# Order of the quarter passes in the retention's score and value products

## The reference

```python
Q, K, V = split_heads(x @ Wq), split_heads(x @ Wk), split_heads(x @ Wv)
G = swish(x @ Wg + bg)
Dmask = gammas[:, None, None] ** maximum(diff, 0.0) * causal
scores = einsum('bhtd,bhsd->bhts', Q, K) / scale
ret = einsum('bhts,bhsd->bhtd', scores * Dmask[None], V)
out = layernorm(ret) * G @ Wo + bo
```

## Time and profile before

| | |
|---|---|
| median of 3 runs | 860.75 us (856.7 to 864.1) |
| profiled execution, span from first to last instruction | 858.2 us |
| its mean granted TensorE clock | 0.968 of full speed |
| PE busy | 786.9 us |
| DVE busy | 556.3 us |
| ACT busy | 331.6 us |
| POOL busy | 241.1 us |
| last stage, eight tiles | from about 597 us to the end |

### The profile page before, as it was taken

The page is one execution under the profiler, slowest core; times in us unless marked ns, Lnnn a source line. Parts: engine busy times, 40 slices in busy tenths (PEclk is TensorE's granted clock), DMA queues, the critical chain, the costliest instruction groups (busy, mean ns, idle before and its releaser), DMA issues.

```text
span 858.2 us, 17840 instructions
## 1 busy us (share of the span) xinstructions
PE 786.9 (92%) x6824; PEld 658.3 (77%) x6824; DVE 556.3 (65%) x1364; ACT 331.6 (39%) x692; POOL 241.1 (28%) x182
## 2 busy tenths in 40 slices
PE   4999999996798988989889999999999999999985
PEld 2798988985687777877778989887877777777742
DVE  6545454548766776567675545458657878787875
ACT  2434645452342332433333434354324334432332
POOL 2431212108655645556453101000211011101010
PEclk9999999997998999999889999999999999999998
DMA  8042333330220211302001011164100000000001
GB/s 277 17 157 80 110 118 105 124 104 0 88 93 28 76 43 64 102 28 76 28 28 54 28 55 28 45 232 159 50 1 1 13 12 12 0 12 12 1 0 37
DMA packets 34101, 53.63 MB, mean 62 GB/s; under 512 B 2561, under 2 KB 23297, under 8 KB 32801
## 3 DMA queue, kind: packets, MB, share of 16 engines
q1 hardware_dynamic: 29168, 36.05, 13.2%
q0 software_dynamic: 3328, 16.78, 5.7%
q10 hardware_dynamic: 1584, 0.53, 0.3%
HBM read 51.19 MB, written 2.16 MB: 62 GB/s over the span
## 4 chain that ended last, share of the span: by engine, by line
PE 74%; issue 11%; DVE 9%; ACT 4%; DMA 1%; DVEq 0%; POOL 0%; POOLq 0%; SPq 0%; ACTq 0%
PE bank L228 47%; PE bank L385 6%; PE bank L394 4%; DVE probs L1069 3%; PE bank L548 3%; PE bank L564 3%; PE bank L513 2%; PE bank L408 2%; ACT probs L676 2%; PE bank L501 2%; ACT kT_high L671 1%; DVE kT_low L1059 1%; PE bank L489 1%; PE bank L557 1%; DMA stage<-in_w_xo 1%
## 5 line engine op out<-in xcount | busy, mean ns | idle before, releaser
L228 PE MATMUL bank<-ctx_high,wk_high 128*128 128x258 f32 x512 | 144.1, 282 | 0.5 <-DVE kT_low L1059 0.5
L228 PE MATMUL bank<-ctx_low,wk_high 128*128 128x258 f32 x512 | 144.3, 282 | 0.0
L228 PE MATMUL bank<-ctx_high,wk_low 128*128 128x258 f32 x512 | 143.9, 281 | 0.0
L1069 DVE TENSOR_SCALAR probs<-probs,rrow 128x257 f32<-128x257 f32 x128 | 120.9, 987 | 2.3
L1059 DVE SCALAR_TENSOR_TENSOR kT_low<-bank,bxk,kT_high 128x258 fp32r<-128x258 f32 x128 | 61.8, 483 | 87.8 <-ACT kT_high L671 87.8
L228 PE MATMUL bank<-wv_high,ctx_high 128*128 128x512 f32 x256 | 110.9, 433 | 0.0
L228 PE MATMUL bank<-wv_low,ctx_high 128*128 128x512 f32 x256 | 105.2, 411 | 0.0
L228 PE MATMUL bank<-wv_high,ctx_low 128*128 128x512 f32 x256 | 104.9, 410 | 0.0
L681 ACT ACTIVATE vals<-bank 128x512 f32<-128x512 f32 x64 | 38.3, 598 | 155.7 <-PE bank L228 155.7
L228 PEld LDWEIGHTS bank<-ctx_high,wk_high 128*128 128x128 f32 x512 | 96.7, 189 | 0.8 <-DVE kT_low L1059 0.7
L228 PEld LDWEIGHTS bank<-ctx_low,wk_high 128*128 128x128 f32 x512 | 96.7, 189 | 0.0
(11 more groups left out here) (206 smaller groups left out, 1657.3 us busy)
## 6 DMA issues: line engine op xcount, KB each, us to landing
raw<-in_ctx_t SPq DMA_DIRECT2D x32, 514.0 KB, 4.0
stage<-in_w POOLq DMA_DIRECT2D x16, 1024.0 KB, 5.9
X<-in_x SPq DMA_DIRECT2D x4, 512.0 KB, 7.2
v_last<-last_values SPq DMA_DIRECT2D x32, 64.0 KB
out<-X SPq DMA_DIRECT2D x8, 256.0 KB, 2.0
stage<-in_w_xq SPq DMA_DIRECT2D x1, 1024.0 KB, 8.5
stage<-in_w_xk SPq DMA_DIRECT2D x1, 1024.0 KB, 13.8
stage<-in_w_xv SPq DMA_DIRECT2D x1, 1024.0 KB, 5.5
```

What stands on the lines that cost most here:

```text
L228: last = pe.matmul(to, left(i, c), right(j, c), start=(c == 0 and i + j == 0), stop=(c == C - 1 and i == 1))
L1069: dve.tensor_scalar(probs[:, g, :], probs[:, g, :], rrow[:, g:g + 1], None, ALU.mult).then_inc(probs_ready, 1)
```

## The change

In `retention_scores` the loop over j goes inside the loop over g, so that consecutive matmuls use different row quarters of the array and different banks, and `s_ready` rises four times at the end, in the round g = 3. The wait for `qkv_kept` (bank 3 free, v kept) that stood before j = 2 stands ahead of all of them. In `retain` the loop over j goes inside too, so that consecutive matmuls use different column quarters, and the four waits for `s_decayed`, one ahead of each group, become one wait for the fourth. The arithmetic of each head is the same.

```diff
--- before.py
+++ after.py
@@ -493,22 +493,22 @@
 
                 pe.wait_ge(tqT_kept, t + 1)
                 pe.wait_ge(tkT_kept, t + 1)
-                for j in range(HG):
-                    if j == 2:
-                        pe.wait_ge(qkv_kept, 3 * t + 3)
-                    rows = slice(DH * j, DH * (j + 1))
-                    for g in range(C):
+                pe.wait_ge(qkv_kept, 3 * t + 3)
+                for g in range(C):
+                    for j in range(HG):
+                        rows = slice(DH * j, DH * (j + 1))
                         last = pe.matmul(bank[S_BANK[j]][:, g * P:(g + 1) * P], tkT[rows, g, :], tqT[rows, g, :],
                                          start=True, stop=True)
-                    last.then_inc(s_ready, 1)
+                        if g == C - 1:
+                            last.then_inc(s_ready, 1)
 
             def retain(t, fed):
 
                 if later(fed):
                     pe.wait_ge(ffn_biased, fed)
-                for j in range(HG):
-                    pe.wait_ge(s_decayed, 4 * t + j + 1)
-                    for g in range(C):
+                pe.wait_ge(s_decayed, 4 * t + 4)
+                for g in range(C):
+                    for j in range(HG):
                         h = HG * g + j
                         last = pe.matmul(bank[7][DH * j:DH * (j + 1), g * P:(g + 1) * P],
                                          v_sb[:, h * DH:(h + 1) * DH], s_sb[:, j, g, :], start=True, stop=True)
```

## The result

The changed kernel takes 873.09 us (median of 4 runs, 871.61 to 874.77) against 861.32 us for the one before (4 runs, one more than stood ahead of the prediction, 856.7 to 864.1): a ratio of 1.0152, 95% interval 1.0112 to 1.0192. It is slower by 1.5%. The prediction said 866.8 us, with a range of 859.5 to 876; its third rival, the clock falling in every tile, said 872.7.

A forecast was written before the change was run, and what follows sets the result against it. The prediction took PE and DVE as two chains of nearly one length, DVE's decays setting the tile. Order 0.2, tiles 1 and 0 +0.1 - 0.1, clock 4.5 + 1.3 made 6.0 us: 866.8 on the 860.75 median; range 859.5 to 876.

The forecast's parts named there:

- third rival: Last stage: the clock falls in every tile, 1.7 us each in loop tiles and tile 1; 872.7 us; chance 0.22.
- What bounds the kernel: Last stage's loop tiles: DVE's row up to the fourth decay, nearly as long as PE's, hangs on nothing PE does earlier.
- Rival 1: Last stage bound by PE alone, so the saving is kept: 23.6 us faster, 837.2 us; chance 0.03.
- The score product: Scores on PE: four row quarters at once, 1.1 us in place of 2.75, a gain that reaches nobody.
- The value product: Values on PE: column quarters overlap, 1.2 us long, next product after 1.1; bounds 1.0 and 1.5 us.
- rival 4: Value product: quarters run only two at a time with 128 moving columns, 2.0 us; 873.4 with the forecast's falls; chance 0.10.
- The new wait: PE ahead of the value product: 3.0 us for the fourth decay, absorbing the saving; +0.04 us a loop tile.
- The clock: Clock falls to half behind the new waits: 1.5 us in 3 of 5 loop tiles, 4.5 us, plus 1.3 in tile 1.
- 2.29 us wait: PE wait ending at 833.22 in the profile before; clock stayed at 1.00, taken as evidence that such a wait does no harm.
- Tile 0: First token tile of the last stage: reckoned 0.1 us earlier, with no clock term.
- Tile 1: Second token tile of the last stage: +0.1 us from order, plus a nearly sure clock fall of 1.3 us.
- Tile 7: Last token tile: clock falls as before, shorter value product at half clock ends at 817.2; no change.

The follow-up runs named there:

- e5: The changed kernel with DVE's four decays moved ahead of the residual's sum and the gate's end: 855.47 us, ratio 0.9941.
- e6: The kernel before, PE's old order kept, with only DVE's four decays moved ahead of the residual's sum and the gate's end: 859.57 us, ratio 0.9983.
- e1: The kernel before with only the score product's half of the change; value product and its four waits as before: 861.14 us, ratio 1.0000.
- e4: The changed kernel with useless matmuls filling PE's waits, 11 ahead of each value product, 7 more in tiles 1 and 7: 859.06 us, ratio 0.9985.
- e9: As e4, but idle matmuls only in tiles 0, 1 and 7, none in the five loop tiles: 866.8 us, ratio 1.0074.
- e12: As e2, with idle matmuls in the waits of tiles 0, 1 and 7 only (5, 11, 11): 865.67 us, ratio 1.0051.
- e2: The kernel before with only the value product's half of the change, including its one wait; scores as before: 873.21 us, ratio 1.0153.
- e3: The kernel before, both products in the old order, only the four waits joined into one for the fourth decay: 873.41 us, ratio 1.0153.
- e11: As e4, but only 5 idle matmuls instead of 11 in each loop tile: 858.78 us, ratio 0.9981.

## Why the prediction came out as it did

**What bounds the kernel.** Right. That DVE's row from the gate product to the fourth decay hangs on nothing that PE now does earlier is what the profile after shows (2.35 and 4.82 us behind the first score). e5 shows that this row bounds the kernel after (28.20 us a tile), e6 that PE's work was as long in the kernel before (29.41). Rival 1, 24 us faster, failed for the reason given.

**The score product** at 1.1 us to the next instruction: 1.10 (669.52 to 670.62). Four row quarters do run together, which no row of before had shown. The gain reached nobody: e1 is at 1.0000, its loop tiles 0.1 us shorter.

**The value product** at 1.1 to 1.2 us: 1.08 at full clock (tile 0, e4). The overlap that the mixing product showed with 32 columns holds with 128, so rival 4 is out.

**The new wait** at 3.0 us: 2.89 in tile 2, 2.90 in the others. The order costs nothing of its own: e4's loop tiles last 29.32 us where the prediction had 29.41 + 0.04.

**The clock.** The mechanism was right, a wait that costs nothing itself and brings the clock down behind it. The size was not: the sum had 6.0 us, and 13.3 came. The step that failed is the count of the falls. One part is "I take 1.5 us for one, and 3 of the 5 loop tiles: 4.5 us". The 1.5 us was right (the loop tiles are 1.34 to 1.56 us longer than before, 1.41 to 1.65 longer than e4's without a fall). All five tiles fell: 7.15 us. The other part is that tile 0, with the same wait, had no term for the clock and no reason given for that, and that tile 7, with longer waits than before, was put at no change since it fell before as well. The prediction took the tiles as independent trials at a wait of uncertain harm, and leaned on the 2.29 us wait that had none behind it; in the kernel after the same wait has a fall. e9 and e12 speak against independent trials: a tile with the same wait can escape, but once one had fallen each later one did. Rival 3 had named this and got 0.22. Its 1.7 us for each fall was a little high, and its 0.5 and 1.0 us for tiles 0 and 7 were low: the table shows 1.5 and 2.6. That the measured time still lies in the stated range is due to this rival, for which the range had been drawn, and not to the sum.

**Tile 0** was reckoned 0.1 us faster; a fall behind its wait of 2.87 us, after the value product, cost it 1.5. **Tile 1** was put at 1.3 + 0.1 and took 1.7. **Tile 7** was put at no change, since it fell before as well. It now waits 2.34 and 2.69 us, and the clock stayed at half twice as long, 824.78 to 831.61; from tile 7 to the end the execution took 2.6 us more. The end holds waits of its own, but most of this is tile 7's: with its two waits filled, the way from its scores to the end takes 49.4 us in e4 and 49.7 in e9, whose loop is otherwise that of the kernel after, against 52.17.

**What the sum missed** is thus 7.15 - 4.7 = 2.45 us in the loop, 1.6 in tile 0, 0.3 in tile 1 and 2.6 behind tile 7, together 6.95. With the sum's 6.0 and the 0.4 us ahead of tile 0, where the programs are the same, that is the 13.3 us between the two spans.

**The third rival's rule.** The rule of the Trainium skill that the prediction quoted (page "TensorE: Matmul & The Clock Gate", section "Why this matters for your kernels", no pause of some microseconds between bursts of matmuls) was a better guide to the count than three tiles in five: the clock fell behind the waits of 2.87 to 2.90 us in all six tiles that had one in the kernel after. The prediction held the harmless wait of 2.29 us against the rule, but the pause of which the page warns is longer than that, so that row said nothing against it. Where the measurements differ from the rule is that the length alone does not decide: a fall stood behind pauses of 1.26 us (e2), and none behind one of 2.89 us (e9, tile 2). The warning of the Trainium skill under "PSUM Bottleneck" in "TensorEngine Tiling (Array Packing)" agrees as well: what empties the score banks bounds the tile, as e5 shows.

## What to carry to other kernels

Where two engines' rows of work are equally long, making one denser gives it a pause, not the kernel a gain; look for what the other engine does in between that nobody is waiting for, and move that first (here the denser order alone cost 1.5%, the earlier decays alone gave 0.2%, which is not clear of nothing, both together 0.6%, and 1.25% with a quarter of the up product moved into the pause). A pause on TensorE is not free even off the bound, since its price is paid by the matmuls behind it; fill it with later work that is ready, and if none is, idle matmuls into a free bank are a cheap test of whether the clock is the cause. In a loop whose tiles are alike do not count such falls as independent chances: the traces here have five of five, four of five in a row, or none.

## What the runs showed of the hardware that I had not expected

- Falls of the clock come in a row: in e9 and e12 tile 2 has the same pause as the others and keeps the clock, and from tile 3 on every tile falls, the falls 30.72 us apart. Whether one brings on the next is not settled.
- The same wait of 2.29 us, behind the same 20 matmuls, had the clock at 1.00 behind it in the kernel before and at 0.50 in the kernel after.
- A pause of 1.26 us was followed by falls (e2, e12), one of 1.26 us was not (e3), and neither was one of 1.74 us behind dense scores (e5) or one of 1.82 us (e11). Ahead of the pause e2 and e3 ran the same instructions; behind it e3's value product took 2.46 us and e2's 1.94 at half clock, 1.08 at full (e12). What separates e2 from e3 is not settled by these runs.
- Four quarters of the array run at once with 128 moving columns, both as row quarters with a bank each (32 score passes in 1.17 us) and as column quarters of one bank (32 value passes in 1.08 us), against 2.82 and 2.46 us with the quarter outermost.
